# A one-core Trainium2 kernel of two MoE passes around a mixer: two router tails, the first mixer pass and a zero store are reordered

## The chip, the cores and the metric

The kernel is one launch on one core of one Trainium2 chip. The metric is device time in microseconds (us). Every number of a trace comes from one profiled execution.

## What is computed

Over 4096 tokens of width 256: `x = x + 0.5 * moe(layernorm(x))`, then `x = x + mixer(layernorm(x))`, then the same MoE again, with the same weights.

```
moe(x):   g = softmax(x @ Wg); s, e = top_k(g, 2); s = s / (sum(s) + 1e-8)
          out = sum_k s_k * ((silu(x @ W11[e_k]) * (x @ W12[e_k])) @ W2[e_k])     # 8 experts, inner width 512
mixer(T): Tn = T / rms(T) * scale; x, z = split(Tn @ in_w.T + in_b); gate = sigmoid(z)
          xc = pointwise(depthwise_conv3(x)); y = ssm(xc) + flip(ssm(flip(xc)))   # 64 states each way
          return T + (y * gate) @ out_w.T + out_b
```

## The kernel before, in words

All engines run programs written out by hand; each waits on semaphores, and within an engine and within a DMA queue the order is the order of the code. The tokens are 8 chunks (`NCH`) of 512 rows, each 4 tiles (`G`) of 128. There are five stages.

*First router, 0 to 68 us.* TensorE computes logits per chunk (`logits_x`) and, one chunk behind, ranks within each expert (`ranks_of`). VectorE takes the top two (`top2_of`) and sums the choices. For each of four groups of two chunks `places_of` (L989) reads the ranks and writes a comparison table `at_place`, the third in chunk 7 of the loop, the fourth inside `router_of`. ScalarE computes variances (`variance_x`), GpSimd turns them into reciprocals (`rsqrt_x`, L488) and normalises the rows of even chunks (its `apply_x`, L596); ScalarE's own `apply_x` (L771) does the odd ones, the last (chunk 7) after its first copy in `tiles_by_p`. SP stores all rows to `xn_rows`. Before them SP stores zeros (L331) from the place named `states`; chunk 2's rows are written to that same place, so GpSimd's `apply_x(2)` waits for the zeros' landing (`pads_out`). In `router_of` VectorE writes for each group n a comparison with the tile number (L1091) and a product (L1093), ScalarE a scaled copy (L711), and TensorE 16 matmuls (L1450). Both tables have two buffers, so group n waits for the matmuls of group n-2. From the result VectorE computes `idx_i` (L1035, L1040), by which GpSimd gathers rows (L550).

*First expert pass, to 419 us, and second, from 606 us.* 71 tiles of 128 rows each, in high and low parts (L1470, L1493). In the first one the results go to `y_rows`.

*First mixer pass, 422 to 511 us.* For each chunk: SP loads both expert outputs (`load_y`, three buffers), VectorE adds them (`sum_choices`, L1231), adds x and computes statistics (`stats_x1`, L1245 and L953) into one of two buffers `xin`, GpSimd computes two reciprocal tables (`rsqrt_rms`, L511: `rstd` for this pass, `x1_rstd` and `x1_mean` for the next), ScalarE normalises (`norm_x1`, L818), TensorE transposes (L1580), ScalarE copies the high part (`rows_high`, L803), VectorE writes the low part (`rows_low`, L1253). Then 36 matmuls (`ssm_in`, L1592), 12 for the gate (L1609), and a scan on VectorE (L1272). In iteration c ScalarE does `rows_high(c+2)`, which waits for `ssm_in(c)`, then `norm_x1(c+3)`, `take_u(c)`, `gate_out(c+1)`; VectorE `rows_low(c+2)`, `stats_x1(c+4)`, the scan of c, `sum_choices(c+5)`; TensorE the transposes of c+2, `ssm_in(c)`, the gate of c+1.

*Second mixer pass, to 577 us, and second router, to 606 us.* Chunks run backwards. The last chunk's logits (`logits_2`, L1672) stand behind a rank group and a `keep_busy` of five matmuls, which compute nothing used. The second router is as the first, with ScalarE's `norm_x2(7)` between its second and third copy (L710), the first three place tables before it and the fourth at the group that needs it. Its rows are stored by SP (L409) behind two pairs of weight loads (L417), and its gathers wait for the landing of all stores of rows.

## Time and profile before

| | us |
|---|---|
| median of 3 runs | 971.47 (970.93 to 971.92) |
| the profiled execution | 969.85 |
| its span | 968.1 |
| TensorE busy | 901.0 (93%) |
| VectorE / ScalarE / GpSimd busy | 582.1 / 391.1 / 577.3 |
| first expert matmul (L1470) starts | 68.13 |

Busy TensorE in the stages, from one view of windows: 47.56 of the first 68 us, 350.00 of the next 354, 74.85 of 89 (422 to 511), 62.96 of 66, 19.93 of 29 (577 to 606), 345.70 of the last 362. The mean granted clock, as a share of full speed, is 0.90, 1.00, 0.94, 1.00, 0.71 and 0.99 in them. In the rows PE is TensorE, DVE VectorE, ACT ScalarE, POOL GpSimd, SPq the DMA issues of SyncE. What stands in brackets at a row's end is how long the engine was idle before it and who released it.

### The profile page before, as it was taken

The page shows a single profiled execution, that of the slowest core. Times are in us where ns is not written, and L with a number is a line of the kernel's source. Part 1 is how long each engine was busy: PE and PEld are TensorE (multiplying, and loading weights), DVE is VectorE, ACT ScalarE, POOL GpSimd, SP SyncE. Part 2 cuts the span into 40 slices and gives each one's busy share as a digit, 9 for nine tenths or more (in the row PEclk, how much of TensorE's full clock was granted, in tenths as well). Part 3 has the DMA queues.
Part 4 walks back from the last instruction along what each step waited for, and adds up shares of the span by engine and source line. Part 5 has one row for each costly group of instructions (what it writes and reads, how often), then busy time and mean ns, then how long its engine had stood idle before and what let it go on. Part 6 is the DMA issues. An engine that isn't in the chain of part 4 may idle for free.

```text
span 968.1 us, 19119 instructions
## 1 busy us (share of the span) xinstructions
PE 901.0 (93%) x5432; PEld 774.1 (80%) x5435; DVE 582.1 (60%) x1385; ACT 391.1 (40%) x768; POOL 577.3 (60%) x614
## 2 busy tenths in 40 slices
PE   7759999999999999968999996999999999999993
PEld 7648888888888888846776874788888888888883
DVE  4876565665666655567736987555555555555551
ACT  3643343443443433305634775333333333333331
POOL 4735666656656665426524653577777777777762
PEclk9979999999999999979999996999999999999997
DMA  9645616436255282167302556744433434343332
GB/s 322 204 152 168 205 55 207 147 111 206 87 174 191 70 275 89 39 196 238 105 0 88 174 163 199 256 99 81 77 54 72 79 51 80 54 75 54 56 44 24
DMA packets 83937, 121.51 MB, mean 126 GB/s; under 512 B 12944, under 2 KB 62736, under 8 KB 83888
## 3 DMA queue, kind: packets, MB, share of 16 engines
q1 hardware_dynamic: 45376, 57.88, 18.4%
q0 software_dynamic: 24992, 37.32, 18.1%
q10 hardware_dynamic: 13520, 25.70, 7.9%
q8 instruction: 24, 0.39, 0.2%
q14 instruction: 25, 0.20, 0.1%
HBM read 73.62 MB, written 47.25 MB: 125 GB/s over the span
## 4 chain that ended last, share of the span: by engine, by line
PE 77%; DVE 7%; POOL 4%; ACT 3%; issue 3%; SPq 2%; DMA 2%; ACTq 1%; POOLq 0%; DVEq 0%
PE bank L1470 40%; PE bank L1493 21%; PE bank L1479 6%; PE bank L1462 3%; PE bank L1592 3%; PE bank L1653 2%; SPq L317 1%; DVE states L1331 1%; SPq L322 1%; ACT work L818 1%; PE bank L1450 1%; DMA out_rows<-yb,idx_i 1%; PE bank L1643 1%; DVE work L1339 1%; POOL work L603 1%
## 5 line engine op out<-in xcount | busy, mean ns | idle before, releaser
L1175 DVE TENSOR_TENSOR sg<-sg,bank 128x512 f32<-128x512 f32 x142 | 97.6, 687 | 281.7 <-ACT sg L747 281.7
L1470 PE MATMUL bank<-w_hi,xt_hi 128*128 x568 | 235.7, 415 | 6.3 <-DVE xt_lo L1164 6.2
L1470 PE MATMUL bank<-w_hi,xt_lo 128*128 x568 | 223.4, 393 | 0.0
L1470 PE MATMUL bank<-w_lo,xt_hi 128*128 x568 | 223.3, 393 | 0.0
L739 ACT ACTIVATE yb<-bank,gates_in 128x256 f32<-128x256 f32 x142 | 67.5, 475 | 313.3 <-PE bank L1493 258.9
L550 POOL DMA_INDIRECT xg<-xn_rows,idx_i x142 | 140.4, 989 | 64.0 <-issue 41.1
L554 POOL DMA_INDIRECT gates_in<-gate_rows,idx_g x142 | 136.4, 960 | 51.6 <-issue 42.7
L1493 PE MATMUL bank<-w_hi,ft_hi 128*128 x568 | 160.1, 282 | 2.2 <-ACT yb L739 2.2
L1493 PE MATMUL bank<-w_lo,ft_hi 128*128 x568 | 160.3, 282 | 0.0
L1493 PE MATMUL bank<-w_hi,ft_lo 128*128 x568 | 160.3, 282 | 0.0
L564 POOL DMA_INDIRECT out_rows<-yb,idx_i x71 | 115.0, 1620 | 60.8 <-ACT yb L739 41.2
L747 ACT ACTIVATE sg<-bank 128x512 f32<-128x512 f32 x142 | 84.8, 597 | 133.3 <-PE bank L1470 126.4
L560 POOL DMA_INDIRECT y_rows<-yb,stat x71 | 72.5, 1021 | 99.0 <-ACT yb L739 95.6
L1470 PEld LDWEIGHTS bank<-w_hi,xt_lo 128*128 128x128 f32 x568 | 106.6, 188 | 23.3
L1470 PEld LDWEIGHTS bank<-w_hi,xt_hi 128*128 128x128 f32 x568 | 107.5, 189 | 21.7 <-issue 8.8
L1470 PEld LDWEIGHTS bank<-w_lo,xt_hi 128*128 128x128 f32 x568 | 107.8, 190 | 12.2
L1493 PEld LDWEIGHTS bank<-w_hi,ft_hi 128*128 128x128 f32 x568 | 107.8, 190 | 8.6 <-issue 3.1
L1493 PEld LDWEIGHTS bank<-w_lo,ft_hi 128*128 128x128 f32 x568 | 107.8, 190 | 6.1
L1493 PEld LDWEIGHTS bank<-w_hi,ft_lo 128*128 128x128 f32 x568 | 107.8, 190 | 0.0
L1170 DVE TENSOR_TENSOR ft_lo<-bank,ft_hi 128x512 fp32r<-128x512 f32 x142 | 96.5, 679 | 3.5 <-ACT ft_hi L729 3.5
L1182 DVE TENSOR_TENSOR fu<-sg,bank 128x512 f32<-128x512 f32 x142 | 96.1, 677 | 0.0
L729 ACT ACTIVATE ft_hi<-bank 128x512 fp32r<-128x512 f32 x142 | 85.1, 599 | 5.8
(288 smaller groups left out, 1297.4 us busy)
## 6 DMA issues: line engine op xcount, KB each, us to landing
w_lo<-w_lo_rows SPq DMA_DIRECT2D x32, 512.0 KB, 4.7
w_lo_rows<-w_lo ACTq DMA_DIRECT2D x16, 512.0 KB
xn_rows<-work SPq DMA_DIRECT2D x14, 512.0 KB, 3.2
seq<-y_rows SPq DMA_DIRECT2D x10, 512.0 KB, 5.2
x_all<-x SPq DMA_DIRECT2D x8, 512.0 KB, 10.3
w_lo_rows<-in_sb ACTq DMA_DIRECT2D x16, 256.0 KB, 2.4
gate<-x SPq DMA_DIRECT2D x16, 256.0 KB, 6.8
seq<-w ACTq DMA_DIRECT2D x7, 512.0 KB, 4.8
```

The source lines that it names most:

```text
L550: nc.gpsimd.indirect_dma_start(xg[t % XG], None, xn_dram, bass.IndirectOffsetOnAxis(ap=idx_i[:, t:t + 1], axis=0)).then_inc(xg_in[t % XG], 16)
L554: nc.gpsimd.indirect_dma_start(gates_in[:, t % XG:t % XG + 1], None, gates_dram, bass.IndirectOffsetOnAxis(ap=idx_g[:, t:t + 1], axis=0)). ...
L560: nc.gpsimd.indirect_dma_start(y_dram, bass.IndirectOffsetOnAxis(ap=idx_s[:, t:t + 1], axis=0), yb[t % 2], None).then_inc(y_out[t % 2], 16)
L564: nc.gpsimd.indirect_dma_start(out, bass.IndirectOffsetOnAxis(ap=idx_i[:, t:t + 1], axis=0), yb[t % 2], None, compute_op=ALU.add).then_inc ...
L729: nc.scalar.activation(ft_hi[p].rearrange("p c k -> p (c k)"), ps_f[:], ACT.Copy).then_inc(ft_hi_ready, 1)
L739: nc.scalar.activation(yb[q % 2], ps_u[:, 0:D], ACT.Copy, scale=gates_in[:, q:q + 1]).then_inc(ye_ready, 1)
L747: nc.scalar.activation(sg[p], ps_g[p][:], ACT.Sigmoid).then_inc(sg_ready, 1)
L1170: nc.vector.tensor_tensor(lo, ps_f[:], hi.bitcast(F32), ALU.subtract).then_inc(ft_ready, 1)
L1175: nc.vector.tensor_tensor(sg[p], sg[p], ps_g[p][:], ALU.mult).then_inc(f_step, 1)
L1182: nc.vector.tensor_tensor(fu[p], sg[p], ps_v[p][:], ALU.mult).then_inc(f_ready, 1)
L1470: last = nc.tensor.matmul(dst[p][:], xt[p][:, c, :], of(w), start=(c == 0 and n == 0), stop=(c == DC - 1 and n == len(parts) - 1))
L1493: last = nc.tensor.matmul(ps_u[:, 0:D], f[p][:, c, :], w, start=(c == 0 and n == 0), stop=(c == IC - 1 and n == len(parts) - 1))
```

## The change

- The zero stores go from SP's queue to GpSimd's, right after its constants.
- GpSimd's `rsqrt_x(7)` comes before its `apply_x(6)`; ScalarE's `apply_x(7)` after its second copy of the first router instead of the first.
- The third place table of the first router is written in `router_of` before the comparison of group 2, not in the chunk loop; the fourth stays before group 3. In the second router the fourth is written before the comparison of group 2 instead of 3.
- For the first two chunks the second half of `load_y` goes to ScalarE's queue.
- The tables for the later pass leave `rsqrt_rms` for a function `table_x1`, run one chunk behind it.
- In the first mixer pass VectorE runs `stats_x1` one chunk further ahead, chunk 4 before the loop; ScalarE runs `norm_x1(c+3)` before `rows_high(c+2)` for c = 1 to 4.
- The last `logits_2` goes ahead of the last but one `ranks_of`, and the five matmuls between them go.

```diff
--- before.py
+++ after.py
@@ -276,6 +276,7 @@
         xn_out = [sem(f"xn_out{b}") for b in range(2)]
         ln_step, mv_ready, rstd_step, rstd_ready, norm_ready = (sem(n) for n in ("ln_step", "mv_ready", "rstd_step", "rstd_ready", "norm_ready"))
         tr_done, xnt_ready, logits_done = (sem(n) for n in ("tr_done", "xnt_ready", "logits_done"))
+        table_step, x1_table = sem("table_step"), sem("x1_table")
         kept, t_ready, res_step, res_ready = (sem(n) for n in ("kept", "t_ready", "res_step", "res_ready"))
         proj_done, xz_ready, states_in = sem("proj_done"), sem("xz_ready"), sem("states_in")
         u_done, u_ready, fwd_done = (sem(n) for n in ("u_done", "u_ready", "fwd_done"))
@@ -326,9 +327,6 @@
             sp.dma_start(wint_sb, wint.rearrange("(c p) n -> p c n", p=P)).then_inc(s_setw, 16)
             sp.dma_start(woutt_sb, woutt).then_inc(s_setw, 16)
 
-            sp.wait_ge(const_ready, 1)
-            for dram in (xn_dram, out):
-                sp.dma_start(dram[L:ROWS, :], zeros).then_inc(pads_out, 16)
             for k in range(NCH):
                 if k == NCH - 2:
                     sp.wait_ge(order_ready, 1)
@@ -374,7 +372,7 @@
             def load_y(i):
 
                 b = y_buffer[i]
-                for k in range(TOPK):
+                for k in range(1 if i < 2 else TOPK):
                     sp.dma_start(y_place[b][k].rearrange("p (j d) -> p j d", d=D),
                                  y_dram[k * L + i * CH:k * L + (i + 1) * CH, :].rearrange("(j p) d -> p j d", p=P)).then_inc(y_in[b], 16)
 
@@ -484,6 +482,9 @@
             nc.gpsimd.iota(p_plus_1, pattern=[[1, 1]], base=1, channel_multiplier=1, allow_small_or_imprecise_dtypes=True)
             nc.gpsimd.iota(tile_of_q[:], pattern=[[1, NT], [NT, TOPK]], base=0, channel_multiplier=0,
                            allow_small_or_imprecise_dtypes=True).then_inc(const_ready, 1)
+            pool.wait_ge(const_ready, 1)
+            for dram in (xn_dram, out):
+                nc.gpsimd.dma_start(dram[L:ROWS, :], zeros).then_inc(pads_out, 16)
 
             def rsqrt_x(k, b):
 
@@ -520,13 +521,17 @@
                 pool.wait_ge(rstd_step, k + 1)
                 nc.gpsimd.tensor_tensor(rstd[:, b, 1, :], vars_[:, b, 1, :], neg_half, ALU.pow).then_inc(r_ready, 1)
                 pool.wait_ge(r_ready, i + 1)
-                pool.wait_ge(kept, i * 4 + 1)
+                pool.wait_ge(kept, 2 * i + 1)
                 nc.gpsimd.tensor_tensor(rstd[:, b, 0, :], x1_mean[:, here], rstd[:, b, 1, :], ALU.mult).then_inc(rstd_ready, 1)
-                pool.wait_ge(kept, i * 4 + 2)
-                nc.gpsimd.tensor_tensor(x1_rstd[:, here], vars_[:, b, 0, :], neg_half, ALU.pow).then_inc(kept, 1)
-                pool.wait_ge(kept, i * 4 + 3)
+            def table_x1(i, b):
+
+                here = slice(i * G, (i + 1) * G)
+                pool.wait_ge(kept, 2 * i + 2)
+                nc.gpsimd.tensor_tensor(x1_rstd[:, here], vars_[:, b, 0, :], neg_half, ALU.pow).then_inc(table_step, 1)
+                pool.wait_ge(table_step, i + 1)
+                pool.wait_ge(rstd_ready, NCH + i + 1)
                 nc.gpsimd.tensor_tensor(x1_mean[:, here], x1_mean[:, here], x1_rstd[:, here], ALU.mult)
-                nc.gpsimd.tensor_scalar(x1_rstd[:, here], x1_rstd[:, here], 1.0, None, ALU.add).then_inc(kept, 1)
+                nc.gpsimd.tensor_scalar(x1_rstd[:, here], x1_rstd[:, here], 1.0, None, ALU.add).then_inc(x1_table, 1)
 
             def residual(i):
 
@@ -603,17 +608,23 @@
                     last = nc.gpsimd.tensor_scalar(xn_x[k % 3][:, t % G, :], x_all[:, t, :], x1_rstd[:, t:t + 1], x1_mean[:, t:t + 1], ALU.mult, ALU.add)
                 last.then_inc(norm_pool, 1)
 
-            for k in range(NCH):
+            for k in range(NCH - 2):
                 rsqrt_x(k, k % 2)
                 if k % 2 == 0:
                     apply_x(k)
+            rsqrt_x(NCH - 2, 0)
+            rsqrt_x(NCH - 1, 1)
+            apply_x(NCH - 2)
             experts(0)
 
             for i in range(NCH):
                 rsqrt_rms(i, i % 2)
+                if i > 0:
+                    table_x1(i - 1, (i - 1) % 2)
+            table_x1(NCH - 1, (NCH - 1) % 2)
 
             pool.wait_ge(s_attw, 64)
-            pool.wait_ge(kept, 4 * NCH)
+            pool.wait_ge(x1_table, NCH)
             pool.wait_ge(norm_ready, NCH)
             for i in range(2):
                 residual(i)
@@ -711,7 +722,7 @@
                     nc.scalar.activation(pair_tile_x[n % 2][:, 0], at_tile[r][n % 2], ACT.Copy, scale=p_plus_1).then_inc(by_p_ready, 1)
                     if r == 1:
                         continue
-                    if n == 0:
+                    if n == 1:
                         apply_x(NCH - 1)
                     if n == NQB - 1:
                         act.wait_ge(norm_pool, NCH // 2)
@@ -825,16 +836,24 @@
                     act.wait_ge(summed, NCH)
                 nc.scalar.activation(seq[:, 0, c * CH + 1:(c + 1) * CH + 1], ps_u1[b][:], ACT.Identity, scale=ssm[:, BBAR:BBAR + 1], bias=ssm[:, UBIAS:UBIAS + 1]).then_inc(u_ready, 1)
 
+            act.wait_ge(lo_out, 32 * E)
+            for p in range(2):
+                act.wait_ge(y_out[p], 16 * ((ET + 1 - p) // 2))
+            for i in range(2):
+                act.dma_start(y_place[y_buffer[i]][1].rearrange("p (j d) -> p j d", d=D),
+                              y_dram[L + i * CH:L + (i + 1) * CH, :].rearrange("(j p) d -> p j d", p=P)).then_inc(y_in[y_buffer[i]], 16)
             for i in range(2):
                 norm_x1(i, i)
                 rows_high(i, i)
             norm_x1(2, 0)
             gate_out(0)
             for c in range(NCH):
+                if 0 < c < NCH - 3:
+                    norm_x1(c + 3, (c + 1) % 2)
                 if c + 2 < NCH:
                     rows_high(c + 2, c % 2)
-                if c + 3 < NCH:
-                    norm_x1(c + 3, (c + 1) % 2)
+                if c == 0:
+                    norm_x1(3, 1)
                 take_u(c, c % 2)
                 if c + 2 < NCH:
                     gate_out(c + 1)
@@ -888,7 +907,7 @@
             act.wait_ge(fwd_done, NCH + 1)
             take_states(0)
             gate_out(NCH - 1)
-            act.wait_ge(kept, 4 * NCH)
+            act.wait_ge(x1_table, NCH)
             norm_t(0)
             take_states(1)
             norm_t(1)
@@ -1075,7 +1094,7 @@
                 link(nc.vector.tensor_scalar(tab["first_16"], small[:, 33:33 + E], -1.0 / P, None, ALU.mult))
                 link(nc.vector.tensor_tensor(tab["picked_first"], onehot, tab["first_16"].unsqueeze(1).unsqueeze(1).to_broadcast([P, TOPK, NT, E]), ALU.mult))
                 link(nc.vector.reduce_sum(tab["first_of_q"].rearrange("p (t k) -> p k t", k=TOPK), tab["picked_first"], AX.X))
-                known = slice(0, NQ - QB) if r == 0 else slice(QB, NQ)
+                known = slice(0, NQ - 2 * QB) if r == 0 else slice(QB, NQ)
                 if r == 0:
                     link(nc.vector.tensor_scalar(pad_rows, place_row[:, 0:ET, 0], -float(P), pad_id, ALU.mult, ALU.add))
                 link(nc.vector.scalar_tensor_tensor(tab["tile"][:, known], tab["whole"][:, known], -1.0 / P, tab["first_of_q"][:, known], ALU.mult, ALU.add))
@@ -1083,9 +1102,12 @@
                     g, b = group_of[r](n), n % 2
                     q = slice(g * QB, (g + 1) * QB)
                     across = lambda a: a[:, q].rearrange("p (t k) -> p t k", k=TOPK).unsqueeze(2).to_broadcast([P, GT, ET, TOPK])
-                    if n == NQB - 1:
-                        places_of(r, n)
-                        link(nc.vector.scalar_tensor_tensor(tab["tile"][:, q], tab["whole"][:, q], -1.0 / P, tab["first_of_q"][:, q], ALU.mult, ALU.add))
+                    late = {(0, 2): [2], (0, 3): [3], (1, 2): [3]}.get((r, n), [])
+                    for m in late:
+                        gm = group_of[r](m)
+                        qm = slice(gm * QB, (gm + 1) * QB)
+                        places_of(r, m)
+                        link(nc.vector.scalar_tensor_tensor(tab["tile"][:, qm], tab["whole"][:, qm], -1.0 / P, tab["first_of_q"][:, qm], ALU.mult, ALU.add))
                     if n >= 2:
                         dve.wait_ge(inv_used, r * (NQB - 1) + n - 1)
                     nc.vector.tensor_tensor(at_tile[r][b], place_row[:, 0:ET, :].unsqueeze(1).to_broadcast([P, GT, ET, TOPK]), across(tab["tile"]), ALU.is_equal).then_inc(oh_ready, 1)
@@ -1218,7 +1240,7 @@
                 top2_of(0, k)
                 if k % 2 == 1:
                     sum_chosen(0, k // 2)
-                if k in (3, 5, 7):
+                if k in (3, 5):
                     places_of(0, (k - 3) // 2)
             router_of(0)
             experts(0)
@@ -1311,14 +1333,14 @@
             rows_low(1, 1)
             stats_x1(3, 1)
             sum_choices(4)
+            stats_x1(4, 0)
             for c in range(NCH):
                 if c + 2 < NCH:
                     rows_low(c + 2, c % 2, last=(c == NCH - 3))
-                if c + 4 < NCH:
-                    stats_x1(c + 4, c % 2)
                 scan_forward(c)
                 if c + 5 < NCH:
                     sum_choices(c + 5)
+                    stats_x1(c + 5, (c + 5) % 2)
             nc.vector.memset(states[N:P, 1, 0:1], 0.0).then_inc(bwd_done, 1)
 
 
@@ -1683,9 +1705,8 @@
                 if i >= 2:
                     ranks_of(1, i - 2)
                 transposes_2(i)
+            logits_2(NCH - 1)
             ranks_of(1, NCH - 2)
-            keep_busy(ps_g[0][:], before.unsqueeze(1).to_broadcast([P, G, P]), 5)
-            logits_2(NCH - 1)
             count(1)
             ranks_of(1, NCH - 1)
             pe.wait_ge(neg_ready, 2 * NCH)

```

## Rows read from the trace of the kernel before

**Rows 1.** Timeline, GpSimd, first router: start us, us, engine, line [idle <- releaser]

```profile
30.28 3.14 POOL L603 TENSOR_SCALAR states<-x_all,stat 128x256 f32<-128x256 f32 x4 [4.86 <-DMA out_rows<-states]
...
44.74 4.09 POOL L603 TENSOR_SCALAR work<-x_all,stat 128x256 f32<-128x256 f32 x4
```

**Rows 2.** Timeline, VectorE, first router.

```profile
37.68 0.27 DVE L996 TENSOR_TENSOR work<-work,bank 128x128 f32<-128x128 bf16 x1
...
40.70 0.06 DVE L1059 MEMSET work<- 128x1 f32 x1
...
44.47 0.76 DVE L1091 TENSOR_TENSOR seq<-place_row,work 128x1136 bf16<-128x1136 bf16 x1
...
46.18 0.73 DVE L1091 TENSOR_TENSOR seq<-place_row,work 128x1136 bf16<-128x1136 bf16 x1
...
51.39 0.28 DVE L996 TENSOR_TENSOR work<-work,bank 128x128 f32<-128x128 bf16 x1
...
56.35 0.75 DVE L1091 TENSOR_TENSOR seq<-place_row,work 128x1136 bf16<-128x1136 bf16 x1 [2.53 <-PE bank L1450]
```

**Rows 3.** Timeline, ScalarE, first router.

```profile
46.48 1.23 ACT L711 ACTIVATE work<-seq,ones_of 128x1136 bf16<-128x1136 bf16 x1
...
50.84 2.07 ACT L776 ACTIVATE work<-x_all,stat 128x256 f32<-128x256 f32 x4 [3.14 <-POOL stat L497]
```

**Rows 4.** Timeline, TensorE, first router.

```profile
54.19 2.05 PE L1450 MATMUL bank<-work,seq 128*128 128x142 bf16 x16 [4.29 <-ACT work L711]
...
58.52 1.81 PE L1450 MATMUL bank<-work,gate 128*128 128x142 bf16 x16 [0.20 <-ACT work L711]
```

**Rows 5.** One chunk: length, busy PE, PEld, DVE, ACT, POOL, clock, DMA, GB/s.

```profile
472.51:481.26 8.75, 8.06 (x38) 6.38 (x39) 7.15 (x19) 5.05 (x10) 4.93 (x8) 1.00 0.01 3
```

**Rows 6.** Waits, TensorE, 456 to 498 us: total us, times, longest.

```profile
PE bank L1580 <- ACT work L818: 2.2, 4, 0.7
```

**Rows 7.** Timeline, ScalarE in the first mixer pass.

```profile
469.41 1.09 ACT L803 ACTIVATE w_lo<-bank 128x512 fp32r<-128x512 f32 x2 [3.66 <-PE bank L1592]
```

**Rows 8.** Timeline, GpSimd at the first gather.

```profile
61.81 1.25 POOL L550 DMA_INDIRECT xg<-xn_rows,idx_i  x1 [11.01 <-DVE idx_i L1035]
```

**Rows 9.** Timeline, VectorE, first mixer pass, third block of low rows.

```profile
453.33 1.29 DVE L1253 TENSOR_TENSOR w_lo<-bank,w_lo 128x512 fp32r<-128x512 f32 x2 [3.10 <-ACT w_lo L803]
```

**Rows 10.** Timeline, ScalarE at its second block of normalised rows.

```profile
440.07 2.07 ACT L818 ACTIVATE work<-work,rstd 128x256 f32<-128x256 f32 x4 [0.41 <-POOL rstd L524]
```

**Rows 11.** The chain that ended last, 412 to 604 us: start us, us, what.

```profile
422.00 4.93 DMA seq<-y_rows
```

**Rows 12.** Timeline, VectorE before the last logits.

```profile
580.45 0.19 DVE L969 COPY logits<-bank 128x32 f32<-128x32 f32 x1 [1.19 <-PE bank L1672]
```

**Rows 13.** Timeline, ScalarE in the second router.

```profile
590.61 2.08 ACT L885 ACTIVATE work<-seq 128x256 f32<-128x256 f32 x4 [0.72 <-POOL seq L509]
...
595.42 1.24 ACT L711 ACTIVATE work<-seq,ones_of 128x1136 bf16<-128x1136 bf16 x1 [1.60 <-DVE seq L1091]
```

**Rows 14.** Timeline, TensorE in the second router.

```profile
593.96 1.24 PE L1450 MATMUL bank<-work,gate 128*128 128x142 bf16 x16 [1.43 <-ACT work L711]
...
596.81 2.05 PE L1450 MATMUL bank<-work,gate 128*128 128x142 bf16 x16 [1.60 <-ACT work L711]
...
605.05 0.38 PE L1462 MATMUL bank<-ident,xg 128*128 128x128 f32 x2
```

**Rows 15.** Timeline, the DMA queue of SP in the second router.

```profile
593.53 0.43 SPq L409 DMA_DIRECT2D xn_rows<-work  x1
```

**Rows 16.** Line 409, 590 to 600 us (one store): issue to landing, us.

```profile
DMA to landing us min/median/max: 6.4/6.4/6.4
```

**Rows 17.** Timeline, GpSimd at the first gather of the second router.

```profile
600.91 1.10 POOL L550 DMA_INDIRECT xg<-xn_rows,idx_i  x1 [10.34 <-DVE idx_i L1040]
```

**Rows 18.** A window after the first router (columns as in rows 5).

```profile
62.00:65.00 3.00, 0.72 (x5) 0.14 (x3) 2.86 (x10) 0.00 (x0) 2.40 (x3) 1.00 0.16 44
```

**Rows 19.** The page's DMA issues: count, KB each, median us to landing.

```profile
x_all<-x SPq DMA_DIRECT2D x8, 512.0 KB, 10.3
```


## The prediction, made before the changed kernel was run

> **What bounds the kernel now.** Read the page first: in the page's table of busy time (shown above) TensorE is busy 93% of the span, so nearly all of the time is the two expert passes, and the diff adds or removes no matmul there. What it can move lies where TensorE waits: the first router (to about 68 us), the first mixer pass (about 422 to 511) and the second router (about 577 to 606). So the timelines of the single engines over these stretches were read next, each wait followed to the engine named as its releaser, then the table of waits and one window of the mixer pass.
>
> In the first router three things hold one another. GpSimd stood 4.86 us before its second block of rows, until the zeros that SP had stored at the end of its load list had landed [rows 1]; ScalarE's variances, which alternate with GpSimd's reciprocals, were late by as much. VectorE made three of four place tables before its router began: the third took 37.68 to 40.70 [rows 2]. And GpSimd worked 4.09 us on a block of rows before the last reciprocal [rows 1], for which ScalarE waited 3.14 us ahead of its second copy for the router's matmuls [rows 3]. TensorE stood 4.29 us before its second group [rows 4], and VectorE then 2.53 us before the fourth [rows 2].
>
> In the mixer pass TensorE is busy 8.06 of 8.75 us in the chunk shown [rows 5]. Its only waits between 456 and 498 us are four before the transposes, 2.2 us in all, for ScalarE's normalised rows [rows 6]. ScalarE stood 3.66 us idle before each turn, for the end of TensorE's long matmuls, and only then copied rows and normalised the next [rows 7].
>
> **First router, part by part.** Zeros: two issues leave SP and two go to GpSimd at about 5 us, where it had nothing to do until 16.7. If they land before GpSimd is ready at 25.4, the 4.86 us wait goes, and with it as much of ScalarE's delay: its first copy for the router could start at 46.48 - 4.83 = 41.65 [rows 1, 3]. What is late next is VectorE. Its third table (3.0 us) leaves the front; TensorE's count, ready only just by then, gives back about 0.4 of it (estimate), so the first comparison starts at 41.8 instead of 44.47. One group costs VectorE 46.18 - 44.47 = 1.71 us, a table with its tile formula 56.35 - 2.53 - 51.39 = 2.43 us [rows 2]. Then: two groups to 45.2, table to 47.65, group to 49.35, table to 51.8, comparison (0.76) to 52.55, ScalarE's copy (1.23) to 53.8, last 16 matmuls at 53.95 instead of 58.52 [rows 3, 4]: 4.57 earlier. ScalarE keeps up: copy, copy, the last block's rows (2.07 us as in [rows 10], its reciprocal now ahead of GpSimd's block), one weight copy, and it is free for the third copy at about 48.6, when VectorE's comparison ends. Against this: the tables and comparisons now fall on GpSimd's last block (the early table took 3.0 us, not 2.43: two of them cost 1.2), and the last group may run all of 2.05 us as the second did, not 1.81 [rows 2, 4]. Ends 3.1 and 4.9; I take 4.1, nearer the undisturbed table, since only the first of the two tables can meet GpSimd's block. From the index to the first expert matmul at 68.13 VectorE works without a gap, and GpSimd's first gather waited for that index alone [rows 8], so the gain stays whole. The stores of rows are issued earlier too and don't end last. The zeros' move and the tables' move overlap: without early zeros about 2.0 of the 4.1 would be left (ScalarE's first copy stays at 46.48, but its third no longer waits 3.14).
>
> A rule of the Trainium skill speaks against the zeros' move: by "SBUF — State Buffer", section "SBUF: two separate sides", a DMA issued on GpSimd's queue has its descriptors written by GpSimd, which VectorE's instructions on the shared port can lock out. No run here shows such a copy of GpSimd's. By the rule the sum stays as it is, since at 5 us VectorE has not begun; were it wrong about when the lock applies, the fourth rival would hold.
>
> **First mixer pass.** (a) ScalarE normalises chunk c+3 before it copies chunk c+2, for c = 1 to 4: its 2.07 us [rows 10] go into the 3.66 us of idle time [rows 7]. The four waits of rows 6 are the transposes of just these chunks, so 2.2 us go; the waits before them, for chunks whose order is unchanged, stay. The cover is the statistics, one chunk further ahead: the extra block is under half of VectorE's 7.15 us per chunk [rows 5] and fits its 3.10 us wait before 453.33 [rows 9], and from there 7.15 us of VectorE fit into the 8.06 that TensorE needs, 0.9 to spare. With that cover gone (a chunk's sum waiting for a load) TensorE would wait for VectorE in place of ScalarE; if half of each wait came back so, 1.1 would be left. (b) The tables for the later pass leave GpSimd's front: ScalarE's second block waited 0.41 for GpSimd [rows 10], the third follows behind it: 0.4. (c) The second halves of the first two expert-output loads go to ScalarE's queue, idle then. The load that ends last took 4.93 us from 422.00 [rows 11], after some 0.4 for the issue before it (estimate, from 421.6 to 422.0); both halves share the same engines, so between -0.3 and 0.4: I take 0.2. Sum 2.2 + 0.4 + 0.2 = 2.8 (1.2 to 3.0).
>
> **Second router.** The last logits go ahead of five filling matmuls and a rank group: VectorE stood 1.19 us for them [rows 12]. ScalarE's first copy comes from its own norm and variance, so nothing starts earlier at 587 to 592. But VectorE's last table (2.43) moves in front of the third comparison, into its waiting there and the 1.19 that the logits give. The fourth comparison then waits only for the second group's matmuls (593.96 - 1.43 = 592.53 [rows 14]) and is done at 593.3; ScalarE is bound by the last norm, which ends at 592.69, then its third copy to 593.9 and its fourth to 595.1 instead of 596.66 [rows 13]: 1.6, and up to 2.4 if the last 16 matmuls run in 1.24 as the group before and not in 2.05 [rows 14]. That is not what comes through. The gather needs the last store of rows too, issued at 593.53 behind weight loads and landing 6.4 later, at 599.93 [rows 15, 16]; the gather started at 600.91 [rows 17]. It can gain 0.6 to 0.7. The first transposes, at 605.05 [rows 14], also waited for six filling matmuls behind VectorE's tables, which come 1.6 earlier, so up to 1.3. Ends 0 and 1.6; I take 0.9, between the two.
>
> **Sum.** 4.1 + 2.8 + 0.9 = 7.8. The profiled execution took 969.85 (span 968.1), so 962.05; the median is 971.47, 1.62 above, so 963.7. Bounds: 4.3 to 9.5, that is 962.0 to 967.2.
>
> **Rivals.**
> 1. *The clock takes part of it back* (15%). After the second router TensorE's ten filling matmuls now start and end up to 2.4 us earlier and, at the higher level, in half the time, so TensorE is idle for some 3 us before the first tile; five more are gone from 577. For: in this very stretch the same 16 matmuls took 1.24 and then 2.05, at 2.4 and 1.2 GHz, after an idle gap of 1.6 us [rows 14]. Against: in another stretch TensorE worked 0.72 of 3 us and the clock stayed full [rows 18]. Price: some 4.8 us at the lower level, as long as the two stretches of rows 14 with the pause between them, cost up to 2.4, of which about 1.4 come through since the first tiles also wait for VectorE, and the 0.9 with it is gone: 963.7 + 2.3 = 966.0. "TensorE: Matmul & The Clock Gate" of the Trainium skill, Part 1, says likewise that a pause lowers the clock and that sustained work raises it again; the trace agrees that it can fall in such a pause.
> 2. *ScalarE's new order brings nothing* (8%): VectorE or the loads become the bound of a chunk. For: 7.15 of 8.06 us is not much room [rows 5]. Against: the loads are due two chunks later than issued. 963.7 + 2.2 = 965.9.
> 3. *The change doesn't do what it says* (6%): both routers end with something that the trace hides behind VectorE, and the pass with its DMA. Then within 0.2%, about 971.
> 4. *Zeros late* (5%), the slower one. The x loads took 10.3 us to land [rows 19]; on GpSimd's queue, for which no row exists under that load, the zeros could come after them. GpSimd's block stands on them, and every us goes through rows 1 and 3 to the first expert tile. Landed at 30.1 as before, 2.0 + 2.8 + 0.9 = 5.7 are gained; from 35.8 on the kernel is slower than before, at 40 us by 4.2: 975.7. Against: they are issued 18 us earlier, and GpSimd's gathers land in about 3 us.
>
> **How the numbers follow.** 66% for the forecast (own range 961.8 to 966). The range 961 to 967.5 takes in rivals 1 and 2 and leaves out 3 and 4 and some of the forecast's edges, about 18%. A change under 0.2% (1.9 us) can't be told from none here. Faster: 0.66 + 0.15 + 0.08 = 0.89; same 0.06; slower 0.05.
>
> **What would show it.** In the trace after: GpSimd's block at 30.28 starts at about 25.5 with no wait for zeros (else rival 4); the router's last 16 matmuls at about 54 and the first expert matmul at about 64; waits before the transposes of the mixer pass near 1 us in all, chunks 8.05 us apart (else rival 2); the gather of the second router ahead of the index only by what the store allows, with the clock full at the first tile (else rival 1). If the zeros land early and the first router still ends after 57 us, the VectorE count is wrong.

## The result and the profile after

| | before | after |
|---|---|---|
| median us | 971.2 (4 runs, 969.46 to 971.92) | 961.17 (4 runs, 960.72 to 961.58) |
| ratio, 95% interval | | 0.9899 (0.9882 to 0.9916) |
| the profiled execution, its span | 969.85, 968.1 | 961.58, 959.8 |
| first expert matmul starts | 68.13 | 63.60 |
| first transposes to ssm_out (the mixer's output matmuls) | 73.89 | 70.37 |
| ssm_out to the second pass' first expert matmul | 95.28 | 94.60 |

963.7 was predicted, with 961.0 to 967.5 as range. The two traces are 8.3 us apart where 7.8 was forecast, the medians 10.0. The 961.17 lie 0.8 us below the lower end that the prediction added up (962.0) and 0.2 us inside the range that it gave.

The GpSimd timeline after, first router (start, length, engine, line, operation; the bracket is idle time and its releaser), which answers to [rows 1]:

```profile
5.24 0.79 POOL L487 DMA_DIRECT2D xn_rows<-states  x1 [0.33 <-POOL tile_of_q L483]
6.04 0.60 POOL L487 DMA_DIRECT2D out_rows<-states  x1
...
25.53 2.23 POOL L608 TENSOR_SCALAR states<-x_all,stat 128x256 f32<-128x256 f32 x4
...
44.79 3.14 POOL L608 TENSOR_SCALAR work<-x_all,stat 128x256 f32<-128x256 f32 x4
```

The zeros cost GpSimd 1.4 us of issuing at a time when it had nothing to do, and the block at 25.53 has no bracket: the 4.86 us are gone. The last block now comes after the last reciprocal and falls on VectorE's first late table.

VectorE's comparisons and the first steps of its tables, answering to [rows 2]:

```profile
41.77 0.75 DVE L1113 TENSOR_TENSOR seq<-place_row,work 128x1136 bf16<-128x1136 bf16 x1
43.22 0.74 DVE L1113 TENSOR_TENSOR seq<-place_row,work 128x1136 bf16<-128x1136 bf16 x1
44.67 0.28 DVE L1015 TENSOR_TENSOR work<-work,bank 128x128 f32<-128x128 bf16 x1
47.62 0.91 DVE L1113 TENSOR_TENSOR seq<-place_row,work 128x1136 bf16<-128x1136 bf16 x1
49.23 0.28 DVE L1015 TENSOR_TENSOR work<-work,bank 128x128 f32<-128x128 bf16 x1
51.71 0.75 DVE L1113 TENSOR_TENSOR seq<-place_row,work 128x1136 bf16<-128x1136 bf16 x1
```

No row has a bracket: VectorE, which had waited 2.53 us before its fourth comparison, works through from 41.77. The first table took 2.95 us (44.67 to 47.62), the second 2.48; the difference is GpSimd's block.

TensorE's four groups of router matmuls and the first expert matmul, answering to [rows 4]:

```profile
43.94 1.23 PE L1472 MATMUL bank<-work,seq 128*128 128x142 bf16 x16 [0.95 <-ACT work L722]
45.39 1.23 PE L1472 MATMUL bank<-work,seq 128*128 128x142 bf16 x16 [0.21 <-ACT work L722]
49.95 2.05 PE L1472 MATMUL bank<-work,gate 128*128 128x142 bf16 x16 [3.33 <-ACT work L722]
53.88 2.05 PE L1472 MATMUL bank<-work,gate 128*128 128x142 bf16 x16 [1.88 <-ACT work L722]
...
63.60 0.50 PE L1492 MATMUL bank<-w_hi,xt_hi 128*128 x1 [1.69 <-DVE xt_lo L1186]
```

Look at the lengths: the same 16 matmuls take 1.23 us twice and, after pauses of 3.33 and 1.88 us, 2.05 us twice; the granted clock is 1.00 for the first two groups and 0.50 for the last two. In the kernel before, the long pauses stood ahead of the first two groups (4.27 and 4.29 us) and the last two had 0 and 0.20; here they stand ahead of the last two.

TensorE's waits after, 430 to 490 us (total, times, longest), answering to [rows 6]:

```profile
PE bank L1602 <- ACT work L829: 3.8, 4, 1.5
```

These four are the transposes of chunks 0 to 3, whose order is as before. The transposes of chunks 4 to 7 wait for nothing; they start 7.86 to 7.94 us apart (458.82, 466.68, 474.55, 482.41) where they were 8.44 to 8.76 apart.

The second router, TensorE with the last logits (line 1694), and windows over them (TensorE busy, ..., the last three: granted clock, share of the DMA engines, GB/s):

```profile
566.10 1.85 PE L1694 MATMUL bank<-wg_sb,work 128*128 128x9 f32 x16
...
570.22 3.13 PE L1694 MATMUL bank<-wg_sb,work 128*128 128x9 f32 x16 [1.17 <-ACT work L885]
```

```profile
568.00:570.00 2.00, 1.05 (x13) 0.81 (x10) 1.86 (x17) 0.91 (x2) 0.20 (x2) 1.00 0.69 239
570.00:572.00 2.00, 1.78 (x11) 1.78 (x11) 1.87 (x5) 2.00 (x5) 0.00 (x0) 0.69 0.13 39
572.00:574.00 2.00, 1.68 (x16) 1.57 (x15) 0.65 (x7) 2.00 (x9) 0.00 (x0) 0.50 0.49 163
```

The same matmuls for the chunk before took 1.85 us. Here they stand behind 1.17 us of idle time that the five filling matmuls had covered, the clock drops to the 1.2 GHz level in their middle, and they take 3.13. VectorE's copy, which was to lose its wait of [rows 12], waits longer:

```profile
573.39 0.19 DVE L988 COPY logits<-bank 128x32 f32<-128x32 f32 x1 [1.32 <-PE bank L1694]
```

The end of the router: SP's queue, answering to [rows 15], the first gather, answering to [rows 17], and the store's landing, to [rows 16]:

```profile
578.67 7.78 SPq L415 DMA_DIRECT2D w_lo<-w_lo_rows  x4
586.49 0.43 SPq L407 DMA_DIRECT2D xn_rows<-work  x1
```

```profile
593.84 1.09 POOL L555 DMA_INDIRECT xg<-xn_rows,idx_i  x1 [10.29 <-DMA xn_rows<-work]
```

```profile
DMA to landing us min/median/max: 6.4/6.4/6.4
```

The index was complete at 592.15, the gather waited for the store: the bound that the prediction named.

### The profile page after: what moved, and what is told of

It reads as the page before. It is cut to its first block, busy times and chain, and to the rows that moved or that the text cites. A ratio compares the mean times of both kernels' runs of the same rounds, so it can differ in the third digit from the quotient of the medians.

```text
span 959.8 us, 19122 instructions
## 1 busy us (share of the span) xinstructions
PE 898.3 (94%) x5429; PEld 773.5 (81%) x5430; DVE 583.2 (61%) x1386; ACT 391.8 (41%) x768; POOL 575.4 (60%) x616
## 4 chain that ended last, share of the span: by engine, by line
PE 81%; DVE 7%; DMA 4%; ACT 2%; issue 2%; POOL 1%; ACTq 1%; POOLq 0%; SPq 0%; DVEq 0%
PE bank L1492 40%; PE bank L1515 21%; PE bank L1501 6%; PE bank L1614 3%; PE bank L1484 3%; PE bank L1430 3%; DMA w_lo<-w_lo_rows 2%; PE bank L1675 2%; PE bank L1631 1%; DVE states L1353 1%; DMA out_rows<-yb,idx_i 1%; PE bank L1665 1%; PE bank L1602 1%; DVE work L1361 1%; ACT work L829 1%
```

## The experiments

They ran on three chips (a, b, c and e on one, f, g, h and k on the second, i, l, m and n on the third), on which the kernel before takes 979 to 982 us instead of 971: there the first expert pass is 4 to 11 us longer, from kernel to kernel by another amount (358 to 364 us from the first expert matmul to the first load of expert outputs; 353.5 before and 353.9 after in the two traces above). So effects of 1 us are read in the stages of the traces and not in the times:

| kernel | first expert matmul | transposes to ssm_out | ssm_out to expert matmul | ratio to before (95%) |
|---|---|---|---|---|
| before | 68.13 | 73.89 | 95.28 | 1 |
| after | 63.60 | 70.37 | 94.60 | 0.9899 |
| n_after_again | 63.57 | 70.34 | 93.60 | 0.9896 (0.9872 to 0.9921) |
| a_zeros_sp | 66.14 | 70.37 | 94.74 | 0.9943 (0.9920 to 0.9966) |
| b_tables_back | 63.83 | 70.38 | 95.74 | 0.9910 (0.9876 to 0.9944) |
| e_before_zeros | 64.31 | 74.69 | 95.21 | 0.9950 (0.9930 to 0.9971) |
| l_rows_order_back | 62.50 | 70.35 | 94.25 | 0.9884 (0.9852 to 0.9917) |
| c_order_back | 63.66 | 72.81 | 94.86 | 0.9930 (0.9905 to 0.9956) |
| f_depth_back | 63.59 | 83.18 | 94.58 | 1.0023 (1.0006 to 1.0041) |
| g_loady_back | 63.60 | 70.34 | 94.59 | 0.9874 (0.9838 to 0.9911) |
| h_busy | 63.78 | 70.38 | 94.10 | 0.9886 (0.9850 to 0.9921) |
| k_logits_back | 63.61 | 70.37 | 93.91 | 0.9906 (0.9871 to 0.9942) |
| i_store_first | 63.64 | 70.38 | 92.81 | 0.9900 (0.9871 to 0.9930) |
| m_short_norms | 63.82 | 70.37 | 92.95 | 0.9891 (0.9867 to 0.9915) |

Where the code is that of the changed kernel the first two stages repeat to 0.25 and 0.05 us; with the mixer pass of before they don't, before and e are 0.80 apart. Nor does the third: the eight kernels with the changed kernel's code there (after, n, a, b, l, c, f, g) lie between 93.60 and 95.74, median 94.6. And an early first tile need not last. TensorE's transposes of the fifth tile's inner rows (line 1501) come 119.75 us after ssm_out in before, and 119.03 in after and in n, 119.04 in g and 119.09 in k, although the first tiles of these four are up to 1.0 us apart.

### The changed kernel again (n_after_again)

> The changed kernel itself, as the one to compare the others of this chip with. Theory (the shares of the edits found in single traces add up): first expert matmul at 63.6, from the first transposes to ssm_out 70.4 us, from ssm_out to the first expert matmul of the second pass 94.6 to 94.9; ratio to the kernel before 0.988 to 0.992. Rival (the first comparison of the two was lucky by the spread of the expert passes): ratio 0.993 or above.

The stages came as expected but for the third, 1.0 quicker, of which nothing is left at the fifth tile. The ratio is 0.9896, so the gain is no accident of one chip.

### Zeros back on SP (a_zeros_sp)

```diff
-            pool.wait_ge(const_ready, 1)
-            for dram in (xn_dram, out):
-                nc.gpsimd.dma_start(dram[L:ROWS, :], zeros)...
+            sp.wait_ge(const_ready, 1)          # at the end of SP's loads
+            for dram in (xn_dram, out):
+                sp.dma_start(dram[L:ROWS, :], zeros)...
```

> The changed kernel with one part undone: the two copies of zeros are issued by SP at the end of its load list again. Theory (overlap): the early zeros and the later tables cover each other, so only part of the 4.5 us of the first router is lost. GpSimd's second block starts at about 30.3 again and ScalarE's first copy at 46.5; the third comparison then waits for TensorE's first group (about 49.2), the table after it and the fourth comparison end at about 54.2, ScalarE's copy at 55.4, and the last 16 matmuls start near 55.5 instead of 53.9: 1.7 lost (1.5 to 2.5), first expert matmul near 65.3. Rival (the zeros pass whole): GpSimd's 4.8 us go through ScalarE to the last matmuls, which start near 58.5, as before the change; 4.5 lost. Time: 963 by the theory, 966 by the rival, against 961.2.

GpSimd's second block waits again:

```profile
30.54 3.21 POOL L608 TENSOR_SCALAR states<-x_all,stat 128x256 f32<-128x256 f32 x4 [5.12 <-DMA out_rows<-states]
```

The first expert matmul is 2.54 later than in the changed kernel and 1.99 earlier than before. The last 16 matmuls start at 56.26, 2.4 later than there. The overlap holds, at the upper edge of the 1.5 to 2.5 that was expected.

### One table back in front (b_tables_back)

```diff
-                if k in (3, 5):
+                if k in (3, 5, 7):
...
-                    late = {(0, 2): [2], (0, 3): [3], (1, 2): [3]}...
+                    late = {(0, 3): [3], (1, 2): [3]}...
```

> The changed kernel with the third place table of the first router back in front of the router (two tables were moved behind the second comparison before, one stays moved). Theory (VectorE's work is only moved): the table costs 2.5 to 3.0 us in front, so the first comparison starts at 44.4 to 44.8 instead of 41.8, but the table behind the second comparison (2.9) is gone, so the third comparison starts at about 47.9 and the fourth at about 51.9 to 52.3 instead of 51.7. Lost: 0.2 to 0.6, the last 16 matmuls near 54.3. Rival (the prediction's own reading, in which the place of the table gave about 2.7 of the 4.1): the last 16 matmuls start at 56 or later, 2 or more lost. Time: 961.7 by the theory, 963.3 by the rival.

Comparisons at 43.81, 45.28, 47.64 and 51.95 instead of 41.77, 43.22, 47.62 and 51.71. The first is 2.0 later, the third not at all: the table's new place gives 0.24 us.

### Zeros alone on the kernel before (e_before_zeros)

```diff
+            pool.wait_ge(const_ready, 1)
+            for dram in (xn_dram, out):
+                nc.gpsimd.dma_start(dram[L:ROWS, :], zeros)...
```

(and the two copies of SP taken out)

> The kernel before the change with one part done: the two copies of zeros issued by GpSimd right after its constants. Theory (with the zeros early everything else in the first router is nearly free): GpSimd's second block starts at 25.5, its last block and the last reciprocal come 4.8 earlier, so ScalarE no longer waits 3.1 us behind its first copy; the first comparison stays at 44.5 (VectorE), the copies start at 45.3 and 46.8, the third comparison at about 48, the fourth at about 52.3; the last 16 matmuls at 54.3 to 54.9 instead of 58.5, 3.6 to 4.2 gained by one part alone. Rival (each part gives its own): the tables' 2.0 are missing, so no more than 2.5 gained, the last 16 matmuls at 56.0 or later. Time: 3.9 under that of before by the theory, 2.3 under by the rival.

The fourth comparison comes at 52.56, 0.85 later than in the changed kernel. The last router group and what TensorE does from there:

```profile
54.73 1.24 PE L1450 MATMUL bank<-work,gate 128*128 128x142 bf16 x16 [0.44 <-ACT work L711]
```

```profile
56.02 2.10 PE L1380 MATMUL bank<-seq,before 128*128 128x512 bf16 x9
60.27 2.37 PE L1380 MATMUL bank<-before 128*128 128x512 bf16 x6 [2.15 <-DVE idx_g L1052]
62.44 0.63 PE L1462 MATMUL bank<-ident,xg 128*128 128x128 f32 x2
```

The group starts 0.85 later than in the changed kernel but runs at 2.4 GHz, 1.24 us, and ends at 55.97, as there (55.93). VectorE's index starts its last step at 56.94; in the changed kernel it was 56.90, before 61.30: this part alone brings all of it. The first expert matmul is at 64.31, 3.82 gained; the other 0.7 is lost behind the index, where the nine filling matmuls end early, TensorE pauses 2.15 us, and the six after it take 2.37 us at the lower clock, where the changed kernel's took 1.46, and the transposes 0.63 for 0.38. That is rival 1 of the prediction, at the first router instead of the second. The pause by itself doesn't explain it: ahead of the same six matmuls TensorE stood idle for 2.28 us in before and for 2.15 in l (below), and there they took 1.46.

### The order of the last rows undone (l_rows_order_back)

```diff
-            for k in range(NCH - 2):
+            for k in range(NCH):
                 rsqrt_x(k, k % 2)
                 if k % 2 == 0:
                     apply_x(k)
-            rsqrt_x(NCH - 2, 0)
-            rsqrt_x(NCH - 1, 1)
-            apply_x(NCH - 2)
...
-                    if n == 1:
+                    if n == 0:
                         apply_x(NCH - 1)
```

> The changed kernel with the order of the last blocks of rows in the first router undone: GpSimd works on its last block before the last reciprocal again, and ScalarE takes its last block behind the first of its copies for the router, not the second. Theory (once the zeros are early this order is worth little): ScalarE's second copy comes at about 47.6 to 48.9 instead of 44.0, the fourth comparison at 51.8 to 52.4 instead of 51.7, first expert matmul 0.1 to 0.7 later, 63.7 to 64.3. Rival (the wait of 3.1 us that stood in the kernel before was a cost of its own): 1.5 us or more later, 65.1.

Neither: the first expert matmul is 1.1 us earlier, at 62.50. TensorE's router groups in this kernel:

```profile
44.31 1.23 PE L1469 MATMUL bank<-work,seq 128*128 128x142 bf16 x16 [1.41 <-ACT work L719]
48.89 2.05 PE L1469 MATMUL bank<-work,seq 128*128 128x142 bf16 x16 [3.35 <-ACT work L719]
50.97 1.55 PE L1469 MATMUL bank<-work,gate 128*128 128x142 bf16 x16
53.61 1.23 PE L1469 MATMUL bank<-work,gate 128*128 128x142 bf16 x16 [1.10 <-ACT work L719]
```

ScalarE waits 1.37 us for GpSimd ahead of its last rows, so the second copy is at 47.52 and the second group at 48.89, next to the third. Two things follow. The pause before the last group is 1.10 us instead of 1.88, and the group takes 1.23 instead of 2.05: 0.82. And GpSimd's block is over before VectorE's tables, which take 2.47 us each, so the fourth comparison is at 51.44 instead of 51.71: 0.27. Together the 1.1.

The pause just ahead of a group doesn't decide its level, though. In n, whose code here is that of the changed kernel, the third group took 1.23 us behind 3.32 us of pause, and only the last 2.05:

```profile
49.92 1.23 PE L1472 MATMUL bank<-work,gate 128*128 128x142 bf16 x16 [3.32 <-ACT work L722]
53.85 2.05 PE L1472 MATMUL bank<-work,gate 128*128 128x142 bf16 x16 [2.70 <-ACT work L722]
```

Windows of after, of n, and two of l (columns as in [rows 5]; the third last is the granted clock):

```profile
48.00:50.00 2.00, 0.05 (x1) 0.08 (x2) 1.90 (x5) 1.60 (x3) 0.00 (x0) 0.63 0.56 183
50.00:52.00 2.00, 1.15 (x16) 0.96 (x15) 1.90 (x6) 0.73 (x1) 0.00 (x0) 0.86 0.97 334
50.00:52.00 2.00, 1.97 (x19) 1.71 (x18) 1.93 (x4) 1.77 (x2) 0.00 (x0) 0.57 0.24 82
52.00:54.00 2.00, 0.90 (x14) 0.74 (x12) 1.93 (x6) 1.77 (x3) 0.00 (x0) 1.00 0.00 0
```

The clock falls ahead of the third group in after and behind it in n; in both TensorE then has single groups between pauses, and the clock is still at 0.50 in the last. In l it has fallen as well, but the second and the third group follow each other (48.89 to 52.52), it comes back within the third, and the last runs at full clock; in e it is the same (50.40 to 54.29). So it is the spreading of the groups that goes with the 0.82. No run moved it alone.

### ScalarE's order in the mixer pass undone (c_order_back)

```diff
-                if 0 < c < NCH - 3:
-                    norm_x1(c + 3, (c + 1) % 2)
                 if c + 2 < NCH:
                     rows_high(c + 2, c % 2)
-                if c == 0:
-                    norm_x1(3, 1)
+                if c + 3 < NCH:
+                    norm_x1(c + 3, (c + 1) % 2)
```

> The changed kernel with ScalarE's order in the first mixer pass undone (it copies rows c+2 before it normalises chunk c+3, for every c); the statistics stay one chunk further ahead. Theory: the transposes of chunks 4 to 7 wait for ScalarE's rows again, 0.4 to 0.7 us each, chunks are 8.5 to 8.8 us apart instead of 7.9, and ssm_out starts 2.2 to 2.9 us later than in the changed kernel (506.2 to 506.9 where the start of the pass is the same). Rival (the gain came from VectorE's statistics being ahead, not from ScalarE's order): chunks stay 7.9 to 8.1 apart and under 1 us is lost. Time: 963.7 by the theory, 961.6 by the rival, against 961.2.

TensorE's waits, 437 to 500 us:

```profile
PE bank L1600 <- ACT work L829: 6.2, 8, 2.1
```

The transposes of chunks 4 to 7 wait again, chunks are 8.43 to 8.54 apart, and the stage takes 2.44 us more. The order gives 2.4 of the pass, and the statistics alone don't.

### The statistics one chunk less ahead (f_depth_back)

```diff
-            stats_x1(4, 0)
             for c in range(NCH):
                 if c + 2 < NCH:
                     rows_low(c + 2, ...)
+                if c + 4 < NCH:
+                    stats_x1(c + 4, c % 2)
                 scan_forward(c)
                 if c + 5 < NCH:
                     sum_choices(c + 5)
-                    stats_x1(c + 5, (c + 5) % 2)
```

> The changed kernel with VectorE's statistics of the first mixer pass back at chunk c+4 in turn c (one chunk less ahead), ScalarE's new order kept. Theory (the extra depth is what the new order stands on): statistics, reciprocal, normalised rows and copied rows of neighbouring chunks form a ring of about 1.1 + 1.5 + 3.0 + 2.0 + 2.1 = 9.7 us, so the chunks 4 to 7 come 9 to 10 us apart instead of 7.9, and from the first transposes to ssm_out the pass takes 4 to 9 us more than the 70.4 us of the changed kernel, more even than the 73.9 of the kernel before. Rival (order alone does it, VectorE and GpSimd are quick enough): chunks 7.9 to 8.1 apart, within 0.8 us of 70.4.

ScalarE's normalised rows, and its waits for GpSimd, 455 to 500 us:

```profile
461.38 2.08 ACT L829 ACTIVATE work<-work,rstd 128x256 f32<-128x256 f32 x4 [4.78 <-POOL rstd L525]
472.97 2.07 ACT L829 ACTIVATE work<-work,rstd 128x256 f32<-128x256 f32 x4 [6.73 <-POOL rstd L525]
484.55 2.08 ACT L829 ACTIVATE work<-work,rstd 128x256 f32<-128x256 f32 x4 [6.72 <-POOL rstd L525]
```

```profile
ACT work L829 <- POOL rstd L525: 24.1, 4, 6.7
```

The ring closes, harder than expected: up to 11.7 us per chunk instead of 9.7, the stage 12.8 longer, the kernel slower than before. The new order without the depth would have been a loss of about 9 us in this stage.

### Loads on one queue again (g_loady_back)

(the second halves' loop on ScalarE's queue taken out, `range(1 if i < 2 else TOPK)` back to `range(TOPK)`)

> The changed kernel with all four of the first two chunks' expert-output loads issued by SP again. Theory (two queues share the same engines and give nothing): from the first issue to VectorE's first sum 5.3 to 5.4 us instead of 5.54, so 0.1 to 0.25 us gained back. Rival (the prediction's term, two queues are 0.2 quicker): 5.7 us or more.

5.39 us from the first issue to the first sum, against 5.59 in after. Over all traces it is 5.36 to 5.41 with one queue (before, e, g, m) and 5.47 to 5.59 with two (the other ten): the second queue costs 0.1 to 0.2.

### Filling matmuls ahead of the last logits (h_busy), and the logits back behind them (k_logits_back)

```diff
+            keep_busy(ps_g[0][:], before..., 5)     # h_busy
             logits_2(NCH - 1)
             ranks_of(1, NCH - 2)
```

```diff
-            logits_2(NCH - 1)
             ranks_of(1, NCH - 2)
+            keep_busy(ps_g[0][:], before..., 5)     # k_logits_back
+            logits_2(NCH - 1)
```

> The changed kernel with five filling matmuls added ahead of the last logits of the second mixer pass, where TensorE is idle for 1.17 us. Theory (the idle time lets the clock fall, and that ate what the logits' earlier place should give): the last logits take 1.85 us instead of 3.13, VectorE's copy of them starts about 1.2 us earlier, so from ssm_out to the first comparison it is 74.0 to 74.4 us instead of 75.5; at the end little of it arrives, since ScalarE's variances of the last chunk wait for a store and its rows for GpSimd: from ssm_out to the first expert matmul 94.2 to 94.6 instead of 94.6 to 94.9. Rival (the clock falls for what came before the idle time): the logits stay at 3 us or more and nothing moves.

> The changed kernel with the last logits of the second mixer pass back behind the rank group and five filling matmuls; the last place table stays in front of the third comparison. Theory (the table's place gives all of the gain, the logits' place gives nothing or costs): the logits take 1.85 us and VectorE's first comparison comes 75.1 us after ssm_out instead of 75.5 to 75.8; from the first comparison to the first expert matmul 19.1 to 19.2 us as in the changed kernel (20.1 before); together 94.2 to 94.6, so 0 to 0.5 us quicker than the changed kernel. Rival (the prediction's reading, the logits' place gives VectorE 1.19 us): 1 us or more slower to the first comparison, 76.4.

| last logits, us | kernels |
|---|---|
| behind the idle time: 3.13, 2.78, 3.44, 2.64, 2.45, 3.43, 3.56, 3.58, 1.95 | after, n, a, b, l, c, f, g, i |
| covered: 1.95, 1.95 | h, m |
| as before: 1.85, 1.85, 1.85 | before, e, k |

With the idle time covered the logits are quick and VectorE's first comparison comes 73.94 us after ssm_out (after: 75.45). The idle time makes slow logits likely, not certain: in i the same 1.17 us stand before them, the clock falls only behind them, and the first comparison comes at 74.04. It stops there: the gather again waits for the store. And h has a cost of its own. 1.2 us into the second pass' first tile the clock falls (two windows, columns as above):

```profile
603.65:604.65 1.00, 0.90 (x4) 0.78 (x5) 0.89 (x4) 0.00 (x0) 0.95 (x1) 1.00 0.92 360
605.65:606.65 1.00, 1.00 (x5) 0.90 (x4) 0.22 (x1) 0.60 (x1) 0.00 (x0) 0.50 1.03 418
```

In b, whose stage is that of the changed kernel, it does so 0.5 us into the tile. By the fifth tile h is 0.4 behind after.

With the logits back and only the table moved, the stage takes 93.91, 1.37 less than before; at the fifth tile it is 0.66 less than before and level with after. So the table's place gave the gain of the second router, 0.7, and the logits' place added nothing at the end, whether the clock falls in them (after) or not (h). That it takes something away there is not shown.

### The store ahead of the second weight load (i_store_first)

```diff
             load_low(0)
-            load_low(1)
             store_xn(NCH - 1)
+            load_low(1)
```

> The changed kernel with the last store of rows ahead of the second load of low weights on SP's queue. Theory (SP was still issuing weight loads when the last rows were ready): the store is issued within 0.2 us of the end of the last norm, where the changed kernel took 0.15 to 0.9; from ssm_out to the first expert matmul 94.0 to 94.5 instead of 94.6. The loads come later, so the wait for them in the first tile may grow from 0.9 to 2 us, which would take it back. Rival (the store's issue was never what held): 94.6 to 94.9 as before.

The store's landing, the gather, and what TensorE waits for in the first tiles, 604 to 620 us:

```profile
DMA to landing us min/median/max: 3.3/3.3/3.3
```

```profile
599.30 1.09 POOL L555 DMA_INDIRECT xg<-xn_rows,idx_i  x1 [7.76 <-DVE idx_i L1059]
```

```profile
PE bank L1492 <- DMA w_lo<-w_lo_rows: 2.1, 2, 1.2
PE bank L1492 <- DVE xt_lo L1186: 0.4, 1, 0.4
```

More than expected: the store is issued at once, but above all it lands in 3.3 us instead of 6.4. The gather waits for the index only and the first tile comes 92.81 us after ssm_out. Part of that is luck, since the logits were quick in this trace; against h, where they were too, it is 1.3. The 2.1 us of waits for weights don't take it back: the changed kernel waits as long in its first tiles, 1.2 for VectorE's rows and 0.9 for weights. At the fifth tile i is still 1.2 ahead of after and n (117.86 after ssm_out for 119.03), at the twelfth 0.1 to 0.4 behind (153.37 for 152.98 and 153.24). What takes it back between these was not tried. In the time nothing is left: 0.9900, n has 0.9896 on the same chip.

### Shorter chain of norms (m_short_norms)

```diff
+            keep_busy(ps_g[0][:], before..., 5)     # ahead of logits_2(NCH - 1)
...
                 if i == NCH:
+                    variance_x2(NCH - 1)            # squares into outw_sb, woc_sb, outb_sb
                 if i >= 2:
                     norm_x2(i - 2)
-            variance_x2(NCH - 1)
```

(with the edits of g and i)

> The changed kernel with four things altered at its loads and in the second mixer pass: all expert-output loads on SP's queue again, five filling matmuls ahead of the last logits, the last store of rows one weight load earlier on SP's queue, and ScalarE's variances of the last chunk ahead of the rows of the chunk before (their squares go into weight buffers that are no longer needed, so they don't wait for a store). Theory (after the table's move the store of the last rows ends the second router, and it is late because norm 6, variance 7, reciprocal 7 and norm 7 stand in a row): the last rows are normalised 1 to 3 us earlier against ssm_out than in the changed kernel (at +77 to +78.5 instead of +79.2 to +79.6), the gather no longer waits for the store but for the index, at about +86.9, and the first expert matmul comes 92.1 to 92.9 us after ssm_out instead of 94.6. Time 1.5 to 2.5 us under the changed kernel, 959. Rival (something else holds the first tile, GpSimd's reciprocals or the low weights): 94 or more.

The last rows are normalised from +77.28 (after: +79.63), as expected, but the gather waits for the index in i already, so this part brings nothing beyond i: 92.95. 971.98 against 971.52 of the changed kernel on the same chip; no version here beats it measurably. l's order with m's stage was not run.

## Why the prediction was right, and where it was not

**In short.** The waits followed in the first two stages and the bound in the third held, and the sum of the traces, 8.3, lies inside the 4.3 to 9.5 that were worked out; the medians' 10.0 don't, and that 961.17 still falls into the range, by 0.2 us, is partly luck.

**First router: 4.53 for 4.1.** Each start was met within 0.1 us (first comparison 41.77 for 41.8, fourth 51.71 for 51.8, last 16 matmuls 53.88 for 53.95 [rows 2, 4]), zeros on GpSimd's queue landed 5.8 to 6.0 us after their issue, long before 25.5, and "without early zeros about 2.0" was 1.99. The doubts held down the sum: the two tables on GpSimd's block were priced at 1.2 and cost 0.5. What the prediction did not see is which edit earns. Its walk through the queue was right as a whole, but a table that leaves the front comes back behind the second comparison: 0.24 (b). The zeros alone bring the index 4.36 us earlier of 4.40 and the first expert matmul 3.82 (e). And the new order of the last rows, whose 3.14 us wait [rows 3] it counted as removed, costs 1.1 (l): with the zeros early the wait is 1.37 and harmless, while the order spreads TensorE's groups apart and lays GpSimd's block over a table. The 2.05 us of the last group stood in the sum as a possible end; that the change's own pauses go with it did not.

**First mixer pass: 3.3 for 2.8,** counted from the first load, above its own upper end of 3.0. (a) 2.2 was 2.44 (c), and its cover is real (f): the depth is worth 12.8 us with this order. (b) 0.4: the first to the fourth transposes took 17.87 us and now take 17.30, in c too, so 0.57 (but 18.72 in e, with the code of before). Another 0.5 lies in the later chunks, 34.40 us from the fourth to the eighth transposes in before and 33.94 in c, for which the sum had no term; no run undid the move of the later pass' tables alone. (c) 0.2 has the wrong sign: it costs 0.1 to 0.2 (g), and the first transposes come 16.08 us after the issue instead of 15.85. The chunks, 7.9 apart for 8.05, were under the floor read from [rows 5]: TensorE is busy for all of the 7.87 us from 466.68, but that is less than its 8.06 before. That transposes without a wait overlap the matmuls around them better would explain it and was not shown. The first expert pass gave 0.44 of the 4.53 back before this stage, in three waits for VectorE's rows (2.1 us before, 2.8 after); why was not tried.

**Second router: 0.7 for 0.9.** The fourth copy came 1.04 earlier for 1.6, counted from ssm_out. The bound by the store was right as the mechanism that stops it in after, n, b, h and k; it is a near tie, and in a, c, f, g and l, with the same code there, the gather waited for the index instead. The step that failed is "the 1.19 that the logits give": without the five filling matmuls the clock fell in the logits in eight traces of nine, and where it held (h) the 1.3 us at the first comparison against k stopped at the store. The bound, taken as given with 6.4 us of landing [rows 16], is made by the weight loads just ahead of the store (i).

**Rivals.** The clock did take something back, but in after and n not where rival 1 put it: at the second pass' first tile it was full. It fell in the last logits and in the last group of the first router, and before the first pass' first tile in e alone. In h and b it fell within the second pass' first tile (windows under h_busy), close to where rival 1 had it. Rival 2's premise, no room on VectorE, failed; rivals 3 and 4 didn't occur.

**What stays open.** The medians are 10.0 us apart (1.01%, in n 1.04%), and the two traces 8.3. The profiled execution of before was 1.35 quicker than its median and that of after 0.4 slower than its own, which is the arithmetic of the gap but no cause. The first expert pass varies by 1.6 to 2.3 us between the traces of one chip, and no run separates that from the change.

## What to carry to other kernels

When several waits stack up in one stage, walk the whole chain with all edits in, then take each edit out: here, in the first router, one of three earned nearly everything and one cost 1.1 us inside a sum that was right. A filling matmul beside a moved step belongs to the step; removing it can cost what the move gains. When a consumer waits for a store, look at what is ahead of it on the queue before taking its landing time as fixed. And follow a gain some tiles further than the first matmul: of four starts that were up to 1.0 us apart nothing was left at the fifth tile.

## What the runs showed of the hardware

The same 16 matmuls of 142 columns take 1.23 us or 2.05 us, and the last group of the first router took 2.05 after pauses of 1.40 to 2.70 us (after, n, a, b, c, f, g, h, i, k, m) and 1.23 to 1.24 after pauses of 0.44 and 1.10 (e, l). The length of that pause is not what decides: the third group took 1.23 to 1.24 us after pauses of 1.99 to 3.33 us in six traces (n, a, b, f, g, i), and in before the last took 1.81 after 0.20. Six matmuls took 1.46 us behind pauses of 2.28 and 2.15 us (before, l) and 2.37 behind 2.15 (e). 16 matmuls of 9 columns behind 1.17 to 1.18 us took 2.45 to 3.58 us in eight traces and 1.95 in one. "TensorE: Matmul & The Clock Gate" of the Trainium skill, Part 1, says that a pause lowers the clock; these rows agree that it falls in such stretches.

A 512 KB store landed in 6.3 to 6.4 us where a pair of 512 KB loads had been issued on its queue 0.8 us before it (eleven traces), in 5.4 where that was 1.5 us before (l), and in 3.4 and 3.3 where it was 5.0 and 7.0 us before (m, i). Two queues for four such loads were not quicker than one, 5.47 to 5.59 against 5.36 to 5.41 us. Two copies of zeros on GpSimd's queue took 0.79 and 0.60 us to issue beside the loads of the two other queues, and landed after 5.8 to 6.0 us; VectorE's first instructions, 0.06 to 0.18 us long, came at 6.14, in the second issue. "SBUF — State Buffer" of the Trainium skill, section "SBUF: two separate sides", warns of VectorE locking out such descriptors, and no run here put such a copy beside longer work of VectorE.
